# Four edits to the engines' order in the feed-forward part of a sandwich block: token split, second product's sum, third softmax group, rounding of the activations

## The chip, the cores and the metric

The program runs on 1 core of one Trainium2 chip. The metric is the device time of the whole program in microseconds (us), as a median of several executions. An execution that was profiled stands beside them, and every row of the trace comes from that one.

## What is computed

Two attention blocks on x of shape (2, 2048, 256), in float32, each with a residual and layer norms around it. The first is plain attention with 16 heads of 16. The second, in which the change lies, is a stack of two layers of this form (cut to what matters):

```python
def _layer(x, wqkv, qs, ksc, wo, lg, lb, w1, b1, w2, b2):
    h = shift_token(x)                       # half of the channels come from the token before
    q, k, v = split(h @ wqkv)                # 8 heads of 64
    q, k = rotary_xpos(l2norm(q) * qs, l2norm(k) * ksc)
    o = local_attention(q, k, v)             # windows of 128, each also sees the window before
    x = x + o @ wo
    h = shift_token(x)
    h = layer_norm(h) * lg + lb
    a, g = split(h @ w1 + b1)                # 682 wide each
    x = x + (a * gelu(g)) @ w2 + b2
    return x

for l in range(2): x = _layer(x, ...)
x = x + _layernorm(...)
```

## The kernel before

The program has a projection phase, the first attention (in which the scores, exponentials and maxima of 32 heads run for most of the first half of the time) and `feed_forward_phase`, which the change edits. It is written engine by engine: each engine has a list of its own, in program order, and semaphores between them. Nothing reorders them: an instruction that waits holds everything behind it on its engine.

The feed-forward phase works on 64 tiles of 128 tokens (32 in each of two layers, the two batches taking turns), as a software pipeline. In step t the engines work on several tiles at once: scores, softmax and attention of tile t+1, projection and rotary embedding of tile t+2, transposed tokens of tile t+3, the layer norm in the middle of tile t, and the hidden products of a pair of tiles. The steps alternate:

- In an **even step** (t even) TensorE makes the hidden layer of a pair, `hidden` (L1307), in two parts; ScalarE takes the gelu of it in six chunks (`gelu`, L1504 and L1506); VectorE multiplies each by the other half (`gated`, L1726); ScalarE rounds the product in two halves (`round_hidden`, L1515), and GpSimd makes the remainders (`split_hidden`, L1102).
- In an **odd step** TensorE makes the second product, `hidden_out` (L1379, L1380, L1386), for both tiles of the pair, and VectorE adds it to x (`add_hidden`, L1665), once early in the step and once at its end.

TensorE's list in a step is: `scores` (L1240), `hidden` chunks 0 to 2 or `hidden_out`, `project` (L1209), `transposed_probs` (L1279, four groups j = 0 to 3 of two heads each), `transposed_hidden_in` (L1255), `hidden` chunks 3 to 5 or `hidden_out`, `outputs_of_heads` (L1321), `transposed_q_k` (L1344), `attended` (L1360), `transposed_x` (L1193). Some of its waits matter here. `transposed_probs` waits for a group to be normalised, and before group 2 for both cosine products of the tile t+2 (`cos_done`, VectorE L1691), since the two share PSUM banks. `hidden_out` of the odd step's second half waits for VectorE's copy of the transposed group 1 (`copy_PT`, L1705). `attended` waits for ScalarE's `copy_oT` (L1520).

The softmax of a tile runs in four groups of 128x512: VectorE adds the mask and takes the maximum (`mask_and_maximum`, L1634), ScalarE the exponential with its sum (L1463), VectorE the reciprocal (`invert_sums`, L1642), and GpSimd (groups 0 and 1, L1054) or VectorE (groups 2 and 3, L1648) multiplies by it. `normalise_mid` (L1684) is the layer norm's scaling on VectorE, from SBUF to SBUF; `mean_and_variance` (L1672 to L1677) before it waits for a DMA that SyncE issues from the finished `x_mid` (L1732), which shifts the tokens by one. `split_xT` (L1653 and L1658) makes the remainder of the transposed tokens from ScalarE's rounded ones (`round_xT`, L1532 and L1534). `sines` (L1075), `inverse_norms` (L1083, L1085), `add_b2` (L1064), `inverse_deviation` (L1059) and `split_y` (L1093, L1095) are on GpSimd. ScalarE's `copy_projected` (L1474, L1475, L1477) gives the projected queries and keys to `sines` and their squares to VectorE.

Of the kernel before, what the change touches and what calls it, by code (L numbers as in the profile page):

```python
# [774 lines left out]
TILES = LAYERS * NT  # L775
# [85 lines left out]
def feed_forward_phase(nc, ins, weights, stacks, division, x_sb, outputs, spare, wo1_loaded, x1_dram, mask_sb, ident, out):  # L861

    with ExitStack() as ctx:
# [93 lines left out]
        exists = lambda v: 0 <= v < TILES  # L957
# [9 lines left out]
        def finished_pair(t):  # L967

            v = t - 5
            return v // 2 if v % 2 == 0 and NT * (LAYERS - 1) <= v < TILES else None  # L970
# [58 lines left out]
        def _(pool):  # L1029
# [31 lines left out]
            def add_b2(v):  # L1061

                pool.wait_ge(x_mid_made, v + 1)
                nc.gpsimd.tensor_tensor(out=x_sb[:, place(v)], in0=x_mid[:, v % 4, 0:2].rearrange("p a c -> p (a c)"), in1=b2_sb[:, layer(v)], op=ALU.add).then_inc(x_b2_made, 1)  # L1064
# [84 lines left out]
            for t in steps:  # L1149
                p = finished_pair(t - 1)  # L1150
                if p is not None:
                    add_x1(p - NT // 2)
                if exists(t + 1):
                    normalise(t + 1, 0)
                    normalise(t + 1, 1)
                if t == -1:
                    outputs_step(PAIRS1 + 1)
                if exists(t):
                    inverse_deviation(t)
                    add_b2(t)  # L1160
                if exists(t + 2):
                    sines(t + 2)
                if t == -1:
                    outputs_step(PAIRS1 + 2)
                if exists(t + 2):
                    inverse_norms(t + 2)
                if exists(t):
                    split_y(t)
                if t % 2 == 0 and exists(t - 2):
                    split_hidden((t - 2) // 2)  # L1170
                if exists(t + 3) and (t + 3) % 2 == 0:
                    rotary_tables((t + 3) // 2)
                p = finished_pair(t)
                if p is not None:
                    last_deviation(p - NT // 2)
# [3 lines left out]
        def _(pe):  # L1179
# [78 lines left out]
            def transposed_probs(v):  # L1258

                hidden_before = v % 2 == 0 and v >= 4  # L1260
                for j in range(4):
                    pe.wait_ge(normed_pool if j < 2 else normed_dve, 2 * v + j % 2 + 1)
                    if j == 0:
                        pe.wait_ge(max_made, 4 * v + 4)
                    if j == 1:
                        if hidden_before:
                            pe.wait_ge(act_made, HC * ((v - 4) // 2) + 5)
                        elif v >= 5:
                            pe.wait_ge(x_new, v - 3)
                        elif v:  # L1270
                            pe.wait_ge(PT_by_dve, 2 * (v - 1) + 1)
                        else:
                            pe.wait_ge(o_normed, 2 * (PAIRS1 - 2))
                    if j >= 2 and exists(v + 1):
                        pe.wait_ge(squares_made, 2 * (v + 1) + 4 - j)
                        pe.wait_ge(cos_done, 2 * (v + 1) + 4 - j)
                    for u in range(2):
                        for kb in key_blocks(v):
                            last = nc.tensor.transpose(bank[PT_BANK[j]][:, (2 * u + kb) * P:(2 * u + kb + 1) * P], probs[j][:, u, kb * P:(kb + 1) * P], ident[:])  # L1279
                    last.then_inc(PT_done, 1)  # L1280
# [172 lines left out]
        def _(act):  # L1453
# [119 lines left out]
            for t in steps:  # L1573
                if exists(t + 1):
                    exponentials(t + 1)
                if t == NT - 1:
                    act.wait_ge(Y_done, NT)
                    weights.load_wo(act, ins, 1)
                if t == NT + 1:
                    weights.load_w1(act, 1)  # L1580
                if t == NT + 2:
                    act.wait_ge(F_done, NT)
                    weights.load_w2(act, 1)
                if t == -1:
                    outputs_step(PAIRS1 + 1)
                if exists(t + 2):
                    copy_projected(t + 2)
                    if t == -1:
                        for k in range(PAIRS1 + 2, PAIRS1 + 5):
                            outputs_step(k)  # L1590
                    if t + 2 == NT - 1:
                        weights.load_second_wqkv(act)
                if exists(t + 1):
                    copy_PT(t + 1)
                if exists(t):
                    affine(t)
                if t % 2 == 0 and exists(t - 2):
                    gelu((t - 2) // 2)
                if exists(t + 1):
                    copy_oT(t + 1)  # L1600
                if exists(t + 2):
                    copy_qT_kT(t + 2)
                if t % 2 == 0 and exists(t - 2):
                    round_hidden((t - 2) // 2, 0)
                if t >= 0 and exists(t + 3):
                    round_xT(t + 3)
                if t % 2 == 0 and exists(t - 2):
                    round_hidden((t - 2) // 2, 1)
                p = finished_pair(t)
                if p is not None:  # L1610
                    normalise_last(p - NT // 2)

        @block.vector
        def _(dve):
# [189 lines left out]
                    scale_keys(0)  # L1804
            for t in steps:
                even, finished = t % 2 == 0, finished_pair(t)
                if exists(t + 1):
                    mask_and_maximum(t + 1, 0)
                    mask_and_maximum(t + 1, 1)
                if t >= 0 and exists(t + 2):  # L1810
                    split_xT(t + 2)
                if exists(t + 1):
                    mask_and_maximum(t + 1, 2)
                    invert_sums(t + 1, 0)
                    mask_and_maximum(t + 1, 3)
                    invert_sums(t + 1, 1)
                if t == -1:
                    outputs_step(PAIRS1 + 1)
                if not even and exists(t - 3):
                    add_hidden(t - 3)  # L1820
                if t == TILES - 1:
                    add_hidden(t - 2)
                if exists(t):
                    mean_and_variance(t)
                if exists(t + 1):
                    for j in (2, 3):
                        invert_sums(t + 1, j)
                        normalise(t + 1, j)
                if t == -1:
                    outputs_step(PAIRS1 + 2)  # L1830
                if exists(t + 2):
                    cosines(t + 2, 1)
                    square_norms(t + 2, 1)
                    cosines(t + 2, 0)
                if t == -1:
                    outputs_step(PAIRS1 + 3)
                    outputs_step(PAIRS1 + 4)
# [118 lines left out]
```

## Time and profile before

| what | value |
|---|---|
| time, median of 3 executions | 2870.36 us (2862.08 to 2893.25) |
| the profiled execution | 2864.45 us, its span 2862.7 us |
| busy TensorE | 2753.9 us, 96% |
| busy VectorE | 2324.5 us, 81% |
| busy ScalarE | 2151.1 us, 75% |
| busy GpSimd | 1133.5 us, 40% |

The feed-forward phase in its steady state begins at about 1640 us from the span's start and ends at about 2820 us. A row of the timeline gives an instruction's start and length; in square brackets stands how long its engine was idle before it, and what ended that. Rows of PEld are TensorE's weight loads, which overlap its matmuls. Line numbers are those of the kernel before.

### The profile page before, as it was taken

The page shows a single profiled execution, that of the slowest core. Times are in us where ns is not written, and L with a number is a line of the kernel's source. Part 1 is how long each engine was busy: PE and PEld are TensorE (multiplying, and loading weights), DVE is VectorE, ACT ScalarE, POOL GpSimd, SP SyncE. Part 2 cuts the span into 40 slices and gives each one's busy share as a digit, 9 for nine tenths or more (in the row PEclk, how much of TensorE's full clock was granted, in tenths as well). Part 3 has the DMA queues.
Part 4 walks back from the last instruction along what each step waited for, and adds up shares of the span by engine and source line. Part 5 has one row for each costly group of instructions (what it writes and reads, how often), then busy time and mean ns, then how long its engine had stood idle before and what let it go on. Part 6 is the DMA issues. An engine that isn't in the chain of part 4 may idle for free. (4 is left out here: it accounts for less than half of the span.)

```text
span 2862.7 us, 60523 instructions
## 1 busy us (share of the span) xinstructions
PE 2753.9 (96%) x22992; PEld 1747.6 (61%) x22992; DVE 2324.5 (81%) x4351; ACT 2151.1 (75%) x4620; POOL 1133.5 (40%) x1307
## 2 busy tenths in 40 slices
PE   7999999999999999999997899999999999999997
PEld 7733333333333333333346788888888888888886
DVE  6779999999999999999917677777777777777774
ACT  5568888888888888888875666677667777777774
POOL 7600000010001000010007666676667767777774
PEclk9979999999999999999999899999999999999999
DMA  5613333434442443344312100000001100000000
GB/s 167 192 18 53 48 51 56 68 60 68 63 75 55 68 63 66 58 74 64 69 32 82 64 5 7 7 6 7 5 7 58 68 14 20 21 21 13 21 19 25
DMA packets 92640, 138.76 MB, mean 48 GB/s; under 512 B 38529, under 2 KB 63041, under 8 KB 84929
## 3 DMA queue, kind: packets, MB, share of 16 engines
q1 hardware_dynamic: 86416, 125.40, 22.1%
q10 hardware_dynamic: 5936, 9.50, 1.0%
q8 instruction: 184, 3.01, 0.5%
q14 instruction: 104, 0.84, 0.1%
HBM read 88.17 MB, written 37.75 MB: 44 GB/s over the span
## 5 line engine op out<-in xcount | busy, mean ns | idle before, releaser
L684 ACT ACTIVATE probs<-scores 128x512 f32<-128x512 f32 x2048 | 1114.3, 597 | 204.0 <-PE scores L610 81.4
L717 DVE TENSOR_REDUCE mx<-aux 128x1 f32<-128x1024 f32 x982 | 1200.8, 1223 | 66.1 <-PE aux L578 58.8
L578 PE MATMUL aux<-k_stack,q_stack 48*128 48x512 f32 x2006 | 751.1, 450 | 14.1 <-DVE mx L725 7.7
L610 PE MATMUL scores<-q_stack,k_stack 50*128 50x512 f32 x2048 | 764.0, 451 | 0.0
L623 PE MATMUL pv<-probs,v_ones 128*32 128x256 f32 x8192 | 659.9, 394 | 0.1
L610 PEld LDWEIGHTS scores<-q_stack,k_stack 50*128 50x128 f32 x2048 | 311.0, 186 | 429.9 <-ACT probs L684 412.4
L623 PEld LDWEIGHTS pv<-probs,v_ones 128*32 128x32 f32 x8192 | 161.9, 108 | 362.0 <-ACT probs L684 288.3
L531 POOL CAST m_parts<-head_max 128x16 fp32r<-128x16 f32 x32 | 6.3, 196 | 877.3 <-DVE head_max L710 877.3
L578 PEld LDWEIGHTS aux<-k_stack,q_stack 48*128 48x128 f32 x2006 | 303.0, 187 | 43.4 <-DVE mx L717 21.3
L1463 ACT ACTIVATE VO<-VO,tables_small 128x256 f32<-128x256 f32 (+1 forms) x512 | 250.5, 491 | 41.4 <-DVE tables_small L1634 41.1
L1307 PE MATMUL bank<-q_minus_first,q_stack 128*128 128x256 f32 x2112 | 271.4, 287 | 2.2 <-POOL q_minus_first L1095 2.2
L1307 PEld LDWEIGHTS bank<-q_minus_first,q_stack 128*128 128x128 f32 x2112 | 259.3, 193 | 12.5 <-issue 9.9
L1209 PE MATMUL bank<-wqkv_hi,k_stack 128*128 128x512 f32 x768 | 253.3, 397 | 7.9 <-DVE tables_small L1634 5.3
L1634 DVE CUSTOM_DVE_ANT_0 VO<-bank,mask_sb,tables_small 128x256 f32<-128x256 f32 (+1 forms) x512 | 216.1, 469 | 52.0 <-PE bank L1240 52.0
L1085 POOL TENSOR_TENSOR tables_small<-tables_small 128x8 f32<-128x8 f32 x128 | 220.8, 1725 | 10.7
L1075 POOL TENSOR_TENSOR VO<-VO,tables_small 128x512 f32<-128x512 f32 x128 | 162.8, 1294 | 91.0 <-issue 90.9
L1054 POOL TENSOR_TENSOR VO<-VO,tables_small 128x512 f32<-128x512 f32 (+1 forms) x128 | 127.2, 1014 | 153.9 <-DVE tables_small L1642 153.9
L1209 PEld LDWEIGHTS bank<-wqkv_hi,k_stack 128*128 128x128 f32 x768 | 145.4, 189 | 40.3 <-issue 5.5
L1732 DVE TENSOR_TENSOR x_mid<-bank,x_sb 128x256 f32<-128x256 f32 x64 | 27.2, 424 | 160.1 <-PE bank L1360 160.1
L1279 PE MATMUL bank<-ident,VO 128*128 128x128 f32 x992 | 126.1, 274 | 29.0 <-DVE VO L1691 28.6
L1209 PE MATMUL bank<-wqkv_lo,k_stack 128*128 128x512 f32 x384 | 152.0, 396 | 0.0
L1102 POOL TENSOR_TENSOR k_stack<-gate,k_stack 128x768 fp32r<-128x768 f32 x64 | 116.8, 1846 | 87.8 <-ACT k_stack L1515 87.8
(178 smaller groups left out, 4559.2 us busy)
## 6 DMA issues: line engine op xcount, KB each, us to landing
q_stack<-qk_dram SPq DMA_DIRECT2D x192, 128.0 KB, 4.9
k_stack<-qk_dram SPq DMA_DIRECT2D x192, 128.0 KB, 6.9
qk_dram<-qkT_hi SPq DMA_DIRECT2D x32, 256.0 KB, 3.6
qk_dram<-qkT_lo SPq DMA_DIRECT2D x32, 256.0 KB, 3.9
w_parts<-weight_pieces SPq DMA_DIRECT2D x28, 256.0 KB, 2.4
VO<-o_stage SPq DMA_DIRECT2D x128, 32.0 KB, 6.9
q_minus_first<-sums_dram SPq DMA_DIRECT2D x32, 128.0 KB, 2.9
x_dram<-x_sb SPq DMA_DIRECT2D x16, 256.0 KB, 2.0
```

The lines of the kernel that those rows point to most:

```text
L578: return nc.tensor.matmul(out, q_stack[max_rows, n % BODY, tile * P:(tile + 1) * P], k_stack[max_rows, n % BODY, keys * 512:(keys + 1) * 512],
L610: last = nc.tensor.matmul(out, k_stack[0:SCORE_ROWS, n % BODY, s * P:(s + 1) * P], q_stack[0:SCORE_ROWS, n % BODY, j * 512:(j + 1) * 512], ...
L623: last = nc.tensor.matmul(pv[VW * j:VW * (j + 1), columns], v_ones[:, n % BODY, s, :], probs[:, (BLOCKS * step + j) % PROBS, columns], sta ...
L684: nc.scalar.activation(probs[:, e % PROBS], scores[:, item_of_exp(e) % BANKS1], ACT.Exp, scale=float(D1) ** -0.5).then_inc(act_emptied, 1)
L717: nc.vector.tensor_reduce(mx[:, n % BODY, tile, half:half + 1], aux[:, unit % 2].rearrange("p a k -> p (a k)"), AX.X, ALU.max).then_inc(dv ...
L1054: nc.gpsimd.tensor_tensor(out=p4, in0=p4, in1=rsums[:, j].unsqueeze(2).to_broadcast([P, 2, P * len(key_blocks(v))]), op=ALU.mult).then_inc ...
L1075: last = nc.gpsimd.tensor_tensor(out=o4[:, :, :, lo:lo + D2 // 2], in0=q4[:, :, :, hi:hi + D2 // 2], in1=sin_table[:, v // 2 % 2, :, lo:lo ...
L1085: nc.gpsimd.tensor_tensor(out=rnorm[:, v % 2, heads], in0=norm2_min[:, heads], in1=minus_half[:, heads], op=ALU.pow).then_inc(rnorm_made, 1)
L1209: last = nc.tensor.matmul(bank[QKV_BANK[a]][:], x_part[:, v % 4, k, tokens], w_part[:, k, columns], start=(k == 0 and n == 0), stop=(k == ...
L1307: last = nc.tensor.matmul(out_half, w_part[:, k, chunk * P:(chunk + 1) * P], h_part[:, p % 2, k], start=(k == 0 and n == 0), stop=(k == NC ...
L1463: last = nc.scalar.activation(probs[j][:, u, keys], probs[j][:, u, keys], ACT.Exp, scale=-1.0, bias=negmax[:, j, u:u + 1], accum_out=sums[ ...
L1634: last = nc.vector.tensor_tensor_reduce(out=probs[j][:, u, at:at + n_keys], in0=src[:, 2 * u * P + at:2 * u * P + at + n_keys], in1=mask_s ...
```

## The change

Four edits of order, one of them with a change of engine:

- `split_xT` of tile t+2 goes in front of all of VectorE's masks and maxima; it stood behind the second of four.
- The first `add_hidden` of an odd step goes behind the two cosine products and the first sum of squares; it stood in front of `mean_and_variance`.
- Group 2 of the softmax is normalised by GpSimd, behind `inverse_deviation`; VectorE keeps group 3 alone. `add_b2` goes behind `sines`.
- Both halves of `round_hidden` go right behind `gelu`, in front of `copy_oT` and the copies of q and k; they stood behind those, the one in front of `round_xT`, the other behind it.

```diff
@@ GpSimd, step t
                 if exists(t):
                     inverse_deviation(t)
-                    add_b2(t)
+                if exists(t + 1):
+                    normalise(t + 1, 2)
                 if exists(t + 2):
                     sines(t + 2)
+                if exists(t):
+                    add_b2(t)
@@ TensorE, transposed_probs
-                    pe.wait_ge(normed_pool if j < 2 else normed_dve, 2 * v + j % 2 + 1)
+                    pe.wait_ge(normed_pool if j < 3 else normed_dve, 3 * v + j + 1 if j < 3 else v + 1)
@@ ScalarE, step t
                     gelu((t - 2) // 2)
+                if t % 2 == 0 and exists(t - 2):
+                    for i in range(2):
+                        round_hidden((t - 2) // 2, i)
                 if exists(t + 1):
                     copy_oT(t + 1)
                 if exists(t + 2):
                     copy_qT_kT(t + 2)
-                if t % 2 == 0 and exists(t - 2):
-                    round_hidden((t - 2) // 2, 0)
                 if t >= 0 and exists(t + 3):
                     round_xT(t + 3)
-                if t % 2 == 0 and exists(t - 2):
-                    round_hidden((t - 2) // 2, 1)
@@ VectorE, step t
+                if t >= 0 and exists(t + 2):
+                    split_xT(t + 2)
                 if exists(t + 1):
                     mask_and_maximum(t + 1, 0)
                     mask_and_maximum(t + 1, 1)
-                if t >= 0 and exists(t + 2):
-                    split_xT(t + 2)
-                if exists(t + 1):
                     mask_and_maximum(t + 1, 2)
                     invert_sums(t + 1, 0)
                     mask_and_maximum(t + 1, 3)
                     invert_sums(t + 1, 1)
-                if not even and exists(t - 3):
+                if t == TILES - 1:
                     add_hidden(t - 3)
-                if t == TILES - 1:
                     add_hidden(t - 2)
                 if exists(t):
                     mean_and_variance(t)
                 if exists(t + 1):
-                    for j in (2, 3):
-                        invert_sums(t + 1, j)
-                        normalise(t + 1, j)
+                    invert_sums(t + 1, 2)
+                    invert_sums(t + 1, 3)
+                    normalise(t + 1, 3)
                 if exists(t + 2):
                     cosines(t + 2, 1)
                     square_norms(t + 2, 1)
                     cosines(t + 2, 0)
+                if not even and t != TILES - 1 and exists(t - 3):
+                    add_hidden(t - 3)
```

The order of three engines at the places in question, with what each instruction waits for. First ScalarE in an even step before, from the last full gelu chunk to the load of the exponentials' table (`k_stack` is here the memory in which the rounded activations and the transposed tokens lie, `VO` holds the keys):

```order
L1504 ACTIVATE gate3<-bank3,b1_sb 128x256 [waits H_done]
L1506 ACTIVATE gate3<-bank4,b1_sb 64x256 [waits H_done]
L1520 COPY oT3<-bank5 128x512 [waits oT_done]
L1525 COPY qT3<-bank6 128x512 [waits qkT_done]
L1527 COPY VO<-bank0 128x512 [waits qkT_done]
L1515 CAST k_stack<-gate3 128x768 [waits F_done,act_made]
L1532 CAST k_stack<-bank2 128x2x128 [waits xT_done]
L1534 CAST k_stack<-bank2 128x1
L1515 CAST k_stack<-gate3 128x768 [waits act_made]
L1463 ACT_TABLE_LOAD
```

The same place of the changed kernel, whose line numbers are 3 higher here:

```order
L1507 ACTIVATE gate3<-bank3,b1_sb 128x256 [waits H_done]
L1509 ACTIVATE gate3<-bank4,b1_sb 64x256 [waits H_done]
L1518 CAST k_stack<-gate3 128x768 [waits F_done,act_made]
L1518 CAST k_stack<-gate3 128x768 [waits act_made]
L1523 COPY oT3<-bank5 128x512 [waits oT_done]
L1528 COPY qT3<-bank6 128x512 [waits qkT_done]
L1530 COPY VO<-bank0 128x512 [waits qkT_done]
L1535 CAST k_stack<-bank2 128x2x128 [waits xT_done]
L1537 CAST k_stack<-bank2 128x1
L1466 ACT_TABLE_LOAD
```

The copy of oT now stands behind two roundings, each of which waits for VectorE's products (`act_made`).

VectorE in an odd step before, from the first `add_hidden` to the copy of the transposed group 1:

```order
L1665 TENSOR_TENSOR x_sb<-bank0,x_sb 128x256 [waits x_b2_made,F_done]
L1672 BN_STATS tables_small3<-x_mid 128x6 [waits shifted1,x_mid_made]
L1672 BN_STATS tables_small3<-x_mid 128x6
L1675 BN_AGGR tables_small3<-tables_small3 128x2 [waits hstats_made]
L1677 TENSOR_SCALAR tables_small3<-tables_small3 128x1 [waits hmv_made]
...
L1648 TENSOR_TENSOR VO<-VO,tables_small3 128x512 [waits rsums3_made]
L1691 TENSOR_TENSOR VO<-bank5,tables_small3 128x512 [waits squares_made,rotary_tables_made]
L1699 TENSOR_REDUCE tables_small3<-VO 128x8 [waits norm2_floor_made,squares_made]
L1691 TENSOR_TENSOR VO<-bank4,tables_small3 128x512 [waits squares_made]
L1684 TENSOR_SCALAR wo1_bo1_sb<-x_mid,tables_small3 128x256 [waits hT_done,hrstd_made]
L1705 COPY PT3<-bank3 128x512 [waits PT_done]
```

And in the changed kernel, whose line numbers are 2 higher here:

```order
L1674 BN_STATS tables_small3<-x_mid 128x6 [waits shifted1,x_mid_made]
L1674 BN_STATS tables_small3<-x_mid 128x6
L1677 BN_AGGR tables_small3<-tables_small3 128x2 [waits hstats_made]
L1679 TENSOR_SCALAR tables_small3<-tables_small3 128x1 [waits hmv_made]
...
L1650 TENSOR_TENSOR VO<-VO,tables_small3 128x512 [waits rsums3_made]
L1693 TENSOR_TENSOR VO<-bank5,tables_small3 128x512 [waits squares_made,rotary_tables_made]
L1701 TENSOR_REDUCE tables_small3<-VO 128x8 [waits norm2_floor_made,squares_made]
L1693 TENSOR_TENSOR VO<-bank4,tables_small3 128x512 [waits squares_made]
L1667 TENSOR_TENSOR x_sb<-bank0,x_sb 128x256 [waits x_b2_made,F_done]
L1686 TENSOR_SCALAR wo1_bo1_sb<-x_mid,tables_small3 128x256 [waits hT_done,hrstd_made]
L1707 COPY PT3<-bank3 128x512 [waits PT_done]
```

The sum with the second product (L1665, now L1667) moved from the head of this stretch to a place between the cosines and the scaling of the layer norm.

GpSimd in an odd step before, from the softmax groups to the inverse norms:

```order
L1054 TENSOR_TENSOR VO<-VO,tables_small3 128x512 [waits rsums3_made] x2
L1059 TENSOR_TENSOR tables_small3<-tables_small3 128x1 [waits var3_made]
L1064 TENSOR_TENSOR x_sb<-x_mid,q_minus_first 128x256 [waits x_mid_made]
L1075 TENSOR_TENSOR VO<-VO,tables_small3 128x16x32 [waits rot3_made,qk3_copied,rotary_tables_made]
L1075 TENSOR_TENSOR VO<-VO,tables_small3 128x16x32
L1083 TENSOR_SCALAR tables_small3<-tables_small3 128x8 [waits norm2_made]
```

And in the changed kernel:

```order
L1054 TENSOR_TENSOR VO<-VO,tables_small3 128x512 [waits rsums3_made] x2
L1059 TENSOR_TENSOR tables_small3<-tables_small3 128x1 [waits var3_made]
L1054 TENSOR_TENSOR VO<-VO,tables_small3 128x512 [waits rsums3_made]
L1075 TENSOR_TENSOR VO<-VO,tables_small3 128x16x32 [waits rot3_made,qk3_copied,rotary_tables_made]
L1075 TENSOR_TENSOR VO<-VO,tables_small3 128x16x32
L1064 TENSOR_TENSOR x_sb<-x_mid,q_minus_first 128x256 [waits x_mid_made]
L1083 TENSOR_SCALAR tables_small3<-tables_small3 128x8 [waits norm2_made]
```

A third product of 128x512 stands ahead of the sines, and the sum with b2 behind them.

## Rows read from the trace of the kernel before

**Rows 1.** Windows view: PE, PEld, DVE, ACT, POOL busy us (instructions), PE clock, DMA share, GB/s.

```profile
1740.00:2000.00 260.00, 254.75 (x2006) 225.03 (x2006) 193.09 (x564) 184.07 (x460) 177.92 (x182) 1.00 0.02 6
```

**Rows 2.** Waits, 1750 to 2750 us: total, times, longest, in us.

```profile
PE bank L1279 <- DVE VO L1691: 17.8, 26, 1.0
...
PEld bank L1379 <- DVE PT L1705: 9.4, 24, 0.4
```

**Rows 3.** Timeline, TensorE, an even step: start, length in us.

```profile
2026.78 1.91 PE L1279 MATMUL bank<-ident,VO 128*128 128x128 f32 x16
...
2035.25 1.89 PE L1360 MATMUL bank<-wo_sb,oT 128*128 128x256 f32 x8
...
2037.29 2.00 PE L1240 MATMUL bank<-VO,qT 64*128 64x256 f32 x16
```

**Rows 4.** Timeline, ScalarE, the same even step and the next step's begin.

```profile
2025.59 0.59 ACT L1474 COPY VO<-bank 128x512 f32<-128x512 f32 x1 [0.30 <-PE bank L1209]
...
2033.02 0.47 ACT L1506 ACTIVATE gate<-bank,b_sb 64x256 f32<-64x256 f32 x1
2034.44 0.59 ACT L1520 COPY oT<-bank 128x512 f32<-128x512 f32 x1 [0.95 <-PE bank L1321]
...
2037.72 0.84 ACT L1515 CAST k_stack<-gate 128x768 fp32r<-128x768 f32 x1
2038.58 1.28 ACT L1463 ACT_TABLE_LOAD   x1
```

**Rows 5.** Timeline, VectorE, the same even step.

```profile
2027.31 0.43 DVE L1684 TENSOR_SCALAR wo_bo_sb<-x_mid,tables_small 128x256 f32<-128x256 f32 x1
...
2031.57 1.26 DVE L1726 SCALAR_TENSOR_TENSOR gate<-bank,b_dve,gate 128x256 f32<-128x256 f32 x3 [0.64 <-ACT gate L1504]
...
2033.36 1.25 DVE L1726 SCALAR_TENSOR_TENSOR gate<-bank,b_dve,gate 128x256 f32<-128x256 f32 x3
```

**Rows 6.** Timeline, TensorE, the odd step behind it.

```profile
2045.65 1.04 PE L1279 MATMUL bank<-ident,VO 128*128 128x128 f32 x8
2047.37 1.07 PE L1279 MATMUL bank<-ident,VO 128*128 128x128 f32 x8 [0.68 <-DVE VO L1691]
2048.27 0.38 PE L1255 MATMUL bank<-ident,wo_bo_sb 128*128 128x128 f32 x2
2048.80 0.39 PE L1379 MATMUL bank<-w_hi,k_stack 128*128 128x256 f32 x1
```

**Rows 7.** Timeline, VectorE, the same odd step.

```profile
2042.56 0.48 DVE L1672 BATCH_NORM_STATS2 tables_small<-x_mid 128x6 f32<-128x128 f32 x2
...
2044.39 1.04 DVE L1648 TENSOR_TENSOR VO<-VO,tables_small 128x512 f32<-128x512 f32 x1
...
2046.54 0.68 DVE L1691 TENSOR_TENSOR VO<-bank,tables_small 128x512 f32<-128x512 f32 x1
2047.14 1.00 DVE L1684 TENSOR_SCALAR wo_bo_sb<-x_mid,tables_small 128x256 f32<-128x256 f32 x1
2048.07 0.68 DVE L1705 COPY PT<-bank 128x512 f32<-128x512 f32 x1
```

**Rows 8.** Timeline, VectorE around the shifting DMA: even step, then odd.

```profile
2016.15 0.42 DVE L1732 TENSOR_TENSOR x_mid<-bank,x_sb 128x256 f32<-128x256 f32 x1 [3.68 <-PE bank L1360]
...
2021.53 0.49 DVE L1672 BATCH_NORM_STATS2 tables_small<-x_mid 128x6 f32<-128x128 f32 x2 [0.25 <-DMA x_mid<-x_mid]
...
2037.18 0.42 DVE L1732 TENSOR_TENSOR x_mid<-bank,x_sb 128x256 f32<-128x256 f32 x1 [2.58 <-PE bank L1360]
```

**Rows 9.** Timeline, GpSimd, the same odd step.

```profile
2041.53 2.04 POOL L1054 TENSOR_TENSOR VO<-VO,tables_small 128x512 f32<-128x512 f32 x2 [0.87 <-DVE tables_small L1642]
...
2044.06 0.82 POOL L1064 TENSOR_TENSOR x_sb<-x_mid,q_minus_first 128x256 f32<-128x256 f32 x1
2045.49 2.50 POOL L1075 TENSOR_TENSOR VO<-VO,tables_small 128x512 f32<-128x512 f32 x2 [0.61 <-issue]
```

**Rows 10.** Timeline, ScalarE, the same odd step.

```profile
2044.79 0.57 ACT L1474 COPY VO<-bank 128x512 f32<-128x512 f32 x1
```

## The prediction, made before the changed kernel ran

> **What bounds the kernel now.** I first read the table of busy time by stretch: in a steady stretch of 260 us TensorE is busy for 254.75, at the full granted clock of 2.4 GHz, and VectorE, the next, for 193.09 [rows 1]. So TensorE's list is the time of this phase, and an edit counts only by what it adds to or takes from TensorE's own waits. The table of waits shows how little there is to take: 17.8 us in 26 places behind VectorE's second cosine product, and 9.4 in 24 places (weight loads) behind VectorE's copy of the transposed group [rows 2]. I then read the timeline of one pair of steps, engine by engine. The pattern repeats through both layers, so two steps carry the whole sum.
>
> In the even step TensorE has no wait: its 16 transposes of the probabilities run through in one piece [rows 3]. In the odd step it stops twice. The last eight of these transposes begin 1.72 us behind the first eight (2045.65 to 2047.37), where half of the even step's uninterrupted piece of 1.91 is about 0.87 with the overlap taken off, which leaves 0.85 of waiting; then the second product begins at 2048.80, 0.53 behind the layer norm's transposes, of which some 0.15 is work, so 0.38 is waiting [rows 3, 6]. Together 1.23 us in each pair is the most that the edits can win, over 31 pairs 38 us.
>
> **Rounding ahead of oT's copy: a new wait in the even step.** The second rounding waits for all six products of `gated`. VectorE ends them at 2033.36 + 1.25 = 2034.61 [rows 5], and what sets that is gelu, which the change leaves where it is. ScalarE ends gelu at 2033.49 [rows 4]. So its new list reads: first rounding 2033.5 to 2034.33 (0.84 each) [rows 4], idle until 2034.65, second rounding to 2035.48, copy of oT (0.59) from about 2035.4 or 2035.5 to 2036.0 or 2036.1. Before, this copy began at 2034.44 and ended at 2035.03 [rows 4], and TensorE began `attended` at 2035.25 straight behind its transposes [rows 3]: 0.22 of slack. With a tenth of a us from ScalarE's end to TensorE's start, `attended` begins at 2036.1 to 2036.2: a loss of 0.82 to 0.95, I take 0.9. Nothing catches it: queued behind `attended` on TensorE are the transposed tokens and the next tile's scores (2037.29) [rows 3], and on VectorE x_mid, the shifting DMA behind it on SyncE's queue and the next masks; all move by as much. The copies of q and k move too, but scores have over a us of their own in hand. The next step's hidden_out gets its rounded input earlier, for which it hardly waits now.
>
> What this edit gives back: the second rounding (0.84) no longer stands between the transposed tokens and the table load of 1.28 [rows 4], so in the odd step, counted from its scores, the exponentials can begin up to 0.5 us earlier and the copy of the queries after them. But that copy can't come earlier than TensorE's projection. In the even step, where it does wait for it, it begins 1.19 ahead of the first transposes (2025.59 against 2026.78) [rows 3, 4]; in the odd step it begins 0.86 ahead (2044.79 against 2045.65) [rows 6, 10]. It can win 0.33 and no more.
>
> **Third group on GpSimd, and the first `add_hidden` behind the cosines.** VectorE loses a product of 128x512 ahead of its cosines (0.68 for one of that size, or 1.04) [rows 7] and the sum, whose like of 128x256 takes 0.42 [rows 8]. With that the second cosine product in the odd step ends about 0.8 to 0.9 us earlier from the scores: it is then bound by ScalarE's squares. This is enough for the first of the two waits, all 0.85 of it. The group itself isn't late: GpSimd's products take 1.02 each [rows 9], the third is done some 0.8 us behind the end of `inverse_deviation`, well over a us ahead of its transposes.
>
> The second wait grows instead. What it waits for is VectorE's chain `normalise_mid`, copy of group 1. `normalise_mid` takes 0.43 in the even step and 1.00 in the odd [rows 5, 7], and in the odd one ends at 2048.14, 0.15 behind GpSimd's sines (2045.49 + 2.50 = 2047.99) [rows 9]. I read this as follows: it can't run beside the second of the two sine instructions and ends when that is over. The sines start 0.13 behind the queries' copy (2044.79 + 0.57 = 2045.36), so by the 0.33 above they move by 0.3 and no more, and `normalise_mid` with them: `add_hidden` now stands directly in front of it and keeps it from slipping in before the second sine instruction begins. Counted from the scores at 2037.29: the queries' copy begins at 7.50 - 0.33 = 7.17 and takes 0.57, their squares as long again, to 8.3; the second cosine product (0.68) ends at 9.0, `add_hidden` at 9.35, when `normalise_mid` could start; the second sine instruction begins at 8.20 - 0.33 + 1.25 = 9.12. So it ends at about 10.5 against 10.85 now, the copy of group 1 as much earlier, and the second product starts 0.35 earlier, not 1.23. If the third product on GpSimd pushes the sines by 0.1, it is 0.25. I take 0.3.
>
> The Trainium skill, in "SBUF — State Buffer", section "Who interferes with whom", says that VectorE in a mode with two ports, or with two SBUF inputs, and GpSimd share a port pair, that whoever starts first has it for the whole instruction, and that the other blocks. The 1.00 and the 1.04 rows agree with it. Taken strictly it would let VectorE's group 3 hold off GpSimd's group 2 by 0.3, with the sines then 0.2 later than I have them; the boundary between the two sine instructions would fall on the very moment at which `normalise_mid` is ready. That is the second rival below, whose price is worked out there from rows.
>
> **`split_xT` in front.** Its cover is VectorE's idle time ahead of the masks; ScalarE's rounding is done early enough. The 0.40 that the masks gain comes to nothing, since `mean_and_variance` waits for the shifting DMA. In the even step it begins 2021.53 - 2016.57 = 4.96 us behind x_mid's end, and waits for it; in the odd step 2042.56 - 2037.60 = 4.96 as well [rows 7, 8]: the DMA is already the last there. So neither this nor `add_hidden`'s removal moves the mean; I cost it at nothing, and if the cover were gone it would cost the 0.40 in one step. `add_b2` (0.82) [rows 9] now stands ahead of the inverse norms, which end about half a us later from the scores; the scaling of the keys on VectorE needs the first of them and is busy until then. In the last layer the final deviation is as much later, and with it x_mid of an odd step, but the even step that follows has no wait on TensorE to lengthen.
>
> **The sum.** A pair: + 0.9 - 0.3 = + 0.6 us. 31 pairs: + 18.6. The first steps, which have no hidden products, wait longer for the cosines and should win 1 or 2 us in all. That makes + 17 us. On the profiled execution's 2864.45 that is 2881.5; the median of the three runs stands 5.9 above that execution, which gives 2887. I name 2884, between them. By the bound of 1%, about what a measurement of this kernel can tell from no change (28.7 us), this is no change, on the slow side.
>
> **The rivals.** (a) *Nothing is won in the odd step.* If VectorE's last product is held by GpSimd's third, as its 1.04 row beside GpSimd's sum with b2 shows it can be [rows 7, 9], the cosines end where they did; or `normalise_mid` waits for sines that come 0.3 later. It decides against me if GpSimd's third product starts before VectorE's. For it: they are within 0.4 us of each other. Against: in the row before, VectorE's started first and kept its length. Then the loss stands alone: 31 x 0.82 to 0.95 = + 25 to + 29, 2890 to 2899. (b) *`normalise_mid` slips in between the sine instructions*, as it does in the even step with 0.43. It misses by 0.2 us by my sum. Then the second wait falls to 0.1 or so, 1.1 is won, and a pair gains 0.2: 31 x 0.2 = - 6, with the first steps - 8, 2856 to 2863. (c) *ScalarE's order costs nothing*, because VectorE's products end sooner than now and oT's copy stays in its slack. Against: gelu sets them. Then the odd step's 0.3 to 1.23 in each pair is all gain: 2826 to 2855. (d) *The new orders stall elsewhere*, in the last layer above all, where GpSimd has most to do: + 30 to + 45, 2894 to 2915.
>
> **Chances.** Forecast (+ 8 to + 24) 0.50, (a) 0.22, (b) 0.17, (c) 0.05, (d) 0.06. The range takes the forecast, (a) and (b): 2856 to 2902; the forecast's own is 2872 to 2894. Over 1% faster is only the far half of (c): 0.03. Over 1% slower is (d) and the upper end of (a) with a median that lies high: 0.15. Within 1%: 0.82.
>
> **What the profile after would show.** Right: in even steps a wait of TensorE in front of `attended` for the copy of oT, some 0.9 us, 31 times; in odd steps no wait for the cosines, and one of 0.7 to 0.9 in front of the layer norm's transposes and the second product; `normalise_mid` at 1 us or more in odd steps; an idle time of 0.6 ahead of the mean, ended by the DMA; a pair of steps at 40.3 us where it is 39.7. Wrong: no such wait in front of `attended`, which would mean that the products end sooner; `normalise_mid` at 0.43 in odd steps, which is (b); or a second cosine product that ends no earlier from the scores than 9.9 us, which is (a).

## The result and the profile after

| | kernel before | changed kernel |
|---|---|---|
| median | 2867.75 us (20 runs) | 2888.09 us (20 runs) |
| ratio | 1 | 1.0071, 95% interval 1.0056 to 1.0085 |
| the profiled execution's span | 2862.7 us | 2884.1 us |

The change makes the kernel slower by 0.7%: some 20 us, 21.4 between the two spans. A ratio is always one of executions in the chip's faster state, which leaves out one of the ten of e3 below (2896.79 us). First the page of the changed kernel, its busy times:

```profile
PE 2767.0 (96%) x22992; PEld 1751.0 (61%) x22992; DVE 2276.4 (79%) x4287; ACT 2155.9 (75%) x4620; POOL 1205.7 (42%) x1371
```

VectorE has 48 us less to do and GpSimd 72 more, with the same instructions on TensorE. None of that says where the time went. The table of waits does (1750 to 2750 us: total, times, longest, in us), against [rows 2]:

```profile
PEld bank L1363 <- ACT oT L1523: 24.8, 25, 1.8
PE bank L1363 <- ACT oT L1523: 18.8, 25, 1.6
...
PEld bank L1258 <- DVE wo_bo_sb L1686: 15.2, 25, 0.9
...
PE bank L1258 <- DVE wo_bo_sb L1686: 9.2, 25, 0.7
PEld bank L1382 <- DVE PT L1707: 9.6, 24, 0.4
```

A wait of TensorE can stand there twice, once for its matmuls (PE) and once for the weight loads ahead of them (PEld); the two are not to be added. The 17.8 us that TensorE waited for the second cosine product are gone but for 0.8. In their place stand two other waits: for oT's copy, once in each even step (25 in this stretch), and for the layer norm's scaling, once in each odd step. The wait for the copy of the transposed group is as it was. The timeline of one even step and the odd step behind it shows them in place, TensorE first, against [rows 3, 6]:

```profile
2039.96 1.09 PE L1347 MATMUL bank<-ident,VO 128*128 128x128 f32 x8
2041.77 1.99 PE L1363 MATMUL bank<-wo_sb,oT 128*128 128x256 f32 x8 [0.72 <-ACT oT L1523]
...
2043.91 2.00 PE L1243 MATMUL bank<-VO,qT 64*128 64x256 f32 x16
...
2052.25 1.97 PE L1282 MATMUL bank<-ident,VO 128*128 128x128 f32 x16
2054.58 0.44 PE L1258 MATMUL bank<-ident,wo_bo_sb 128*128 128x128 f32 x2 [0.35 <-DVE wo_bo_sb L1686]
...
2062.36 2.00 PE L1243 MATMUL bank<-VO,qT 64*128 64x256 f32 x16
```

`attended` (L1363) begins 1.81 us behind the transposes of q and k, where it was 0.92 (2034.33 to 2035.25). The odd step's 16 transposes now run in one piece, but the layer norm's begin 2.33 behind them, where the even step needs 1.75. ScalarE in the same even step, against [rows 4]:

```profile
2038.65 0.47 ACT L1509 ACTIVATE gate<-bank,b_sb 64x256 f32<-64x256 f32 x1
2039.15 0.83 ACT L1518 CAST k_stack<-gate 128x768 fp32r<-128x768 f32 x1
2040.27 0.83 ACT L1518 CAST k_stack<-gate 128x768 fp32r<-128x768 f32 x1 [0.30 <-DVE gate L1728]
2041.13 0.58 ACT L1523 COPY oT<-bank 128x512 f32<-128x512 f32 x1
```

The first rounding follows gelu almost at once, the second waits 0.30 us for VectorE's last products, and oT's copy, whose input was there at 2039.96 or so, starts at 2041.13. Then the odd step, VectorE and GpSimd, against [rows 5, 7, 9]:

```profile
2049.16 0.49 DVE L1674 BATCH_NORM_STATS2 tables_small<-x_mid 128x6 f32<-128x128 f32 x2 [0.61 <-DMA x_mid<-x_mid]
...
2050.29 0.69 DVE L1650 TENSOR_TENSOR VO<-VO,tables_small 128x512 f32<-128x512 f32 x1
...
2052.33 0.68 DVE L1693 TENSOR_TENSOR VO<-bank,tables_small 128x512 f32<-128x512 f32 x1
2052.93 0.41 DVE L1667 TENSOR_TENSOR x_sb<-bank,x_sb 128x256 f32<-128x256 f32 x1
2053.26 1.26 DVE L1686 TENSOR_SCALAR wo_bo_sb<-x_mid,tables_small 128x256 f32<-128x256 f32 x1
2054.44 0.68 DVE L1707 COPY PT<-bank 128x512 f32<-128x512 f32 x1
```

```profile
2050.67 1.21 POOL L1054 TENSOR_TENSOR VO<-VO,tables_small 128x512 f32<-128x512 f32 x1
2051.85 2.53 POOL L1075 TENSOR_TENSOR VO<-VO,tables_small 128x512 f32<-128x512 f32 x2
2054.32 0.78 POOL L1064 TENSOR_TENSOR x_sb<-x_mid,q_minus_first 128x256 f32<-128x256 f32 x1
```

The cosines end 9.1 us behind the scores (2053.01 - 2043.91) where they ended 9.9 behind. The sum takes its 0.41, and the scaling (L1686) starts at 2053.26, when the second sine instruction has just begun (2051.85 + 1.26 = 2053.11, half of the row). It lasts 1.26 us and ends 0.14 behind the sines.

I took the start of every tile's scores from the two timelines. From the first step with hidden products on, 28 of the 30 even steps are 0.98 us longer than before, and 28 of the 30 odd ones shorter by 0.22 to 0.30: 22.02 for 21.04 and 18.45 for 18.70. All 30 even steps together are longer by 29.9, the 30 odd ones shorter by 7.4, and the first three steps shorter by 1.4. That makes 21.1 us between the first scores and the last.

The two odd ones out among the even steps: at the border of the two layers one loses 1.96 instead of 0.98. Its tile is the first of a batch and sees one block of keys only, and the wait for oT's copy is the longest there (1.6 on TensorE); that oT is ready earlier against gelu in such a tile is my reading. And one step loses only 0.44, since the kernel before lost 0.54 in it (21.58 for 21.04). There the layer norm's scaling began 0.03 us before the end of the first sine instruction and waited out the second, for 1.41 us instead of the even step's 0.43.

### The profile page after: what moved, and what is told of

Its sections match the earlier page's. It is cut to its first block and busy times, and to the rows that moved or that the text cites. A ratio compares the mean times of both kernels' runs of the same rounds, so it can differ in the third digit from the quotient of the medians.

```text
span 2884.1 us, 60523 instructions
## 1 busy us (share of the span) xinstructions
PE 2767.0 (96%) x22992; PEld 1751.0 (61%) x22992; DVE 2276.4 (79%) x4287; ACT 2155.9 (75%) x4620; POOL 1205.7 (42%) x1371
## 5 line engine op out<-in xcount | busy, mean ns | idle before, releaser
L1054 POOL TENSOR_TENSOR VO<-VO,tables_small 128x512 f32<-128x512 f32 (+1 forms) x192 | 201.2, 1061 | 191.9 <-DVE tables_small L1644 191.7
L1085 POOL TENSOR_TENSOR tables_small<-tables_small 128x8 f32<-128x8 f32 x128 | 241.9, 1890 | 10.7
L1363 PE MATMUL bank<-wo_sb,oT 128*128 128x256 f32 x512 | 125.5, 388 | 23.8 <-ACT oT L1523 23.8
L1693 DVE TENSOR_TENSOR VO<-bank,tables_small 128x512 f32<-128x512 f32 x128 | 88.0, 688 | 62.8 <-ACT VO L1478 57.6
```

What stands on the lines that cost most here:

```text
L1054: nc.gpsimd.tensor_tensor(out=p4, in0=p4, in1=rsums[:, j].unsqueeze(2).to_broadcast([P, 2, P * len(key_blocks(v))]), op=ALU.mult).then_inc ...
L1085: nc.gpsimd.tensor_tensor(out=rnorm[:, v % 2, heads], in0=norm2_min[:, heads], in1=minus_half[:, heads], op=ALU.pow).then_inc(rnorm_made, 1)
L1363: last = nc.tensor.matmul(bank[Y_BANK][:, 0:C], oT[:, c], wo_sb[:, c], start=(c == 0), stop=(c == 3))
```

## The experiments

Each variant was timed against the kernel before on the same chip: e1 to e4 on one, where that took 2868.06 us, e5 to e8 on another, where it took 2865.70. So compare ratios, not times. e2, e4, e7 and e8 have 4 executions, the others 10. "Steps" are the distances between the scores of successive tiles in the profiled execution, even and odd.

A ratio of so few executions is blunt beside an edit worth a few us, for much of the spread arises ahead of the changed phase: the first scores begin between 1550.9 us (e8) and 1565.7 (e2), and the mean granted clock in the first 1550 us is 0.99 in the one and 0.97 in the other. From 1600 to 2750 us it is 1.00 in every profile. So the time from the first scores to the last, read in each profile, shows the edits more sharply:

| kernel | first scores to last, us | against before |
|---|---|---|
| before | 1252.4 | |
| changed | 1273.5 | + 21.1 |
| e1 | 1251.5 | - 0.9 |
| e2 | 1275.2 | + 22.8 |
| e3 | 1243.4 | - 8.9 |
| e4 | 1217.6 | - 34.8 |
| e5 | 1249.4 | - 3.0 |
| e6 | 1244.7 | - 7.7 |
| e7 | 1217.4 | - 35.0 |
| e8 | 1231.5 | - 20.9 |

**e1: roundings back.** All of the change but ScalarE's part:

```diff
-                if t % 2 == 0 and exists(t - 2):
-                    for i in range(2):
-                        round_hidden((t - 2) // 2, i)
                 if exists(t + 1):
                     copy_oT(t + 1)
                 if exists(t + 2):
                     copy_qT_kT(t + 2)
+                if t % 2 == 0 and exists(t - 2):
+                    round_hidden((t - 2) // 2, 0)
                 if t >= 0 and exists(t + 3):
                     round_xT(t + 3)
+                if t % 2 == 0 and exists(t - 2):
+                    round_hidden((t - 2) // 2, 1)
```

> The changed kernel with ScalarE's list as before (both roundings behind the copies again); the other three edits stay. Theory (the wait for oT's copy is the whole loss, and the 0.24 us won in odd steps came from ScalarE's side): no wait in front of the attended product, an even step of 21.03 us, and an odd step of 18.69, because the queries' copy and with it the sines come where they came before; only the first steps win. So 0.999 of the kernel before, 0.992 of the changed one. Rival (GpSimd's third product and the blocked scaling make the loss): 1.005 or more of the kernel before. Second rival (the two VectorE edits win the odd step by themselves): odd steps of 18.4, 0.996.

Measured: 0.9994 (0.9971 to 1.0016), steps 21.04 and 18.71. Both rivals fall: without ScalarE's edit nothing is lost, and VectorE's and GpSimd's edits win nothing by themselves. The odd step's wait is in front of the transposes again, for the second cosine product, as in the kernel before (waits of this kernel, 1750 to 2750 us):

```profile
PE bank L1282 <- DVE VO L1694: 22.2, 26, 0.9
```

The lighter list of VectorE did not bring the cosines forward here, and VectorE's and GpSimd's timelines of an odd step show why:

```profile
2044.62 1.47 DVE L1651 TENSOR_TENSOR VO<-VO,tables_small 128x512 f32<-128x512 f32 x1
```

```profile
2044.51 1.04 POOL L1054 TENSOR_TENSOR VO<-VO,tables_small 128x512 f32<-128x512 f32 x1
```

ScalarE's exponentials come later than in the changed kernel, and VectorE waits 0.44 us for the sums of the last group. GpSimd's third product then starts first, by 0.11 us, and VectorE's takes 1.47 us instead of 0.69. This is the mechanism of the forecast's rival (a), and it comes in every odd step of this kernel in which a tile sees two blocks (1.45 to 1.49 us). The second cosine product ends 10.1 us behind the scores, where it ended 9.9 behind. The sines start 8.20 behind the scores, as before, so the scaling ends where it did.

**e2: roundings alone.** The kernel before with only ScalarE's edit (the diff above, read backwards).

> The kernel before with the roundings in front of oT's copy as the only edit. Theory: even steps of 22.02 us (+ 0.99), and odd steps won 0.25 to 0.35 by the earlier sines although VectorE's list is as before, since the scaling of the layer norm ends with the sines either way: 1.007 to 1.008 of the kernel before, the same as the changed kernel. Rival (the odd step is won by VectorE's shorter list): odd steps stay at 18.69, 1.011.

Measured: 1.0091 (1.0061 to 1.0120), steps 22.02 and 18.50. The loss of the even step is whole with this edit alone, and 0.20 of the odd step's gain comes with it, although VectorE's list is that of before. The ratio lies a little above my 1.008, within its interval. The odd step of this kernel on VectorE and on GpSimd:

```profile
2065.34 0.81 DVE L1683 TENSOR_SCALAR wo_bo_sb<-x_mid,tables_small 128x256 f32<-128x256 f32 x1
2066.07 0.68 DVE L1704 COPY PT<-bank 128x512 f32<-128x512 f32 x1
```

```profile
2063.28 2.71 POOL L1075 TENSOR_TENSOR VO<-VO,tables_small 128x512 f32<-128x512 f32 x2 [0.22 <-issue]
```

The scaling ends at 2066.15, again 0.16 behind the sines (2065.99).

**e3: one rounding ahead.** The changed kernel, but only the first rounding stands ahead of oT's copy; the second stands behind the copies of q and k:

```diff
                 if t % 2 == 0 and exists(t - 2):
-                    for i in range(2):
-                        round_hidden((t - 2) // 2, i)
+                    round_hidden((t - 2) // 2, 0)
                 if exists(t + 1):
                     copy_oT(t + 1)
                 if exists(t + 2):
                     copy_qT_kT(t + 2)
+                if t % 2 == 0 and exists(t - 2):
+                    round_hidden((t - 2) // 2, 1)
                 if t >= 0 and exists(t + 3):
                     round_xT(t + 3)
```

> The changed kernel with only the first rounding in front of oT's copy; the second goes behind the copies of q and k and in front of the tokens' rounding. Theory: the first rounding ends before oT is there, so the wait goes (even step 21.03), while the exponentials' table load still comes early and the odd step keeps its 0.24 (18.45): 31 x 0.24 and the first steps, 0.996 to 0.997 of the kernel before. Rival (oT's copy is late by the first rounding too, or the tokens' rounding is now late): even steps of 21.3 or more, 1.000 or above.

Measured: 0.9968 (0.9949 to 0.9986), steps 21.04 and 18.44. As the theory had it. From 1750 to 2750 us TensorE waits for oT once, for 0.3 us, at the border of the layers. There the first rounding alone is in the way of oT's copy too, and the step takes 19.54 us instead of 18.84.

**e4: one rounding ahead, late sum.** As e3, with the first `add_hidden` of an odd step moved once more (VectorE's list, cut to what matters):

```diff
                     cosines(t + 2, 0)
-                if not even and t != TILES - 1 and exists(t - 3):
-                    add_hidden(t - 3)
                 if exists(t):
                     normalise_mid(t)
                 if exists(t + 1):
                     copy_PT(t + 1, 1)
                 if exists(t + 2):
                     square_norms(t + 2, 0)
                 if exists(t + 1):
                     copy_PT(t + 1, 3)
+                if not even and t != TILES - 1 and exists(t - 3):
+                    add_hidden(t - 3)
```

> As the one before, and the first add_hidden of an odd step stands behind the copy of the transposed group 3, no longer between the cosines and the layer norm's scaling. Theory (the scaling is stuck behind the second sine instruction because it comes 0.15 us too late): it now starts before that instruction, takes 0.3 to 0.45 us, and the second wait of the odd step goes as well: odd steps of 17.5 to 17.8 us, 0.984 to 0.988 of the kernel before. Rival (the scaling takes 1.0 to 1.26 in odd steps whenever the sines run, wherever it starts): odd steps of 18.4, as the one before.

Measured: 0.9888 (0.9853 to 0.9923), median 2839.72 us, steps 21.03 and 17.6 in the first layer, 17.5 in the second. The steps are those of the theory. The ratio lies just above the 0.984 to 0.988 that I expected, with most of that range inside its interval, and the 34.8 us between the scores are 1.2%. The scaling now starts before the first of the two sine instructions is over, on VectorE and GpSimd (an odd step, whose scores began at 2021.74):

```profile
2030.16 0.68 DVE L1694 TENSOR_TENSOR VO<-bank,tables_small 128x512 f32<-128x512 f32 x1
2030.75 0.40 DVE L1687 TENSOR_SCALAR wo_bo_sb<-x_mid,tables_small 128x256 f32<-128x256 f32 x1
2031.17 0.69 DVE L1708 COPY PT<-bank 128x512 f32<-128x512 f32 x1
```

```profile
2029.67 2.62 POOL L1075 TENSOR_TENSOR VO<-VO,tables_small 128x512 f32<-128x512 f32 x2
```

It takes 0.40 us where it took 1.26, and TensorE runs from its transposes into the second product without a wait:

```profile
2030.10 1.95 PE L1282 MATMUL bank<-ident,VO 128*128 128x128 f32 x16
2031.89 0.38 PE L1258 MATMUL bank<-ident,wo_bo_sb 128*128 128x128 f32 x2
2032.02 0.37 PE L1382 MATMUL bank<-w_hi,k_stack 128*128 128x256 f32 x1
```

**e5: late sum, both roundings ahead.** The changed kernel with the sum moved as in e4.

> The changed kernel with both roundings in front of oT's copy, and the first add_hidden of an odd step behind the copy of the transposed group 3. Theory (the two waits are independent): even steps of 22.02 us as in the changed kernel, odd steps of 17.5 to 17.6: a pair is 0.1 us shorter than before, 0.995 to 0.997 of the kernel before. Rival (the early input of the second product, or something else that the roundings' place brings, is needed for the short odd step, or the late one spoils it): odd steps of 18 or more, 1.001 or above.

Measured: 1.0006 (0.9983 to 1.0029), steps 22.02 and 17.5 to 17.6. The steps are those of the theory; the two waits are independent, and each edit adds its own. The wait for oT in the even step costs here nearly all that the late sum wins in the odd one. My ratio of 0.995 to 0.997 did not follow from my own steps: 0.1 us in 31 pairs and the first steps are some 4 us, 0.998 to 0.999. Between the first scores and the last 3.0 us are won, 0.999, because the border of the layers loses 3.6 us (22.40 for 18.84). In that step the eight matmuls of `attended` take 3.40 us behind their wait, for a cause that I did not look for.

**e6: third group back on VectorE**, on top of e4 (cut; TensorE's waits for the groups go back with it):

```diff
# GpSimd
-                if exists(t + 1):
-                    normalise(t + 1, 2)
# VectorE
-                    invert_sums(t + 1, 2)
-                    invert_sums(t + 1, 3)
-                    normalise(t + 1, 3)
+                    for j in (2, 3):
+                        invert_sums(t + 1, j)
+                        normalise(t + 1, j)
```

> The fast variant (one rounding ahead, late sum) with group 2 normalised by VectorE again. Theory: VectorE's 0.62 us more ahead of the cosines bring the layer norm's scaling to 9.6 us behind the scores, past the begin of the second sine instruction at 9.1, so it is stuck to 10.4 again: odd steps of 18.3 to 18.45, 0.997 of the kernel before. Rival (the third group on GpSimd does nothing, the late sum is all): odd steps of 17.6, 0.989.

Measured: 0.9988 (0.9966 to 1.0010), steps 21.04 and 18.36 in the first layer, 18.5 in the second; the 7.7 us won between the scores are the 0.997 expected. So the third group on GpSimd is worth about 0.8 to 1.0 us in an odd step on top of e4: without it the scaling comes too late again. VectorE's scaling and GpSimd's sines in an odd step of this kernel are

```profile
2008.77 1.02 DVE L1685 TENSOR_SCALAR wo_bo_sb<-x_mid,tables_small 128x256 f32<-128x256 f32 x1
```

```profile
2007.13 2.52 POOL L1075 TENSOR_TENSOR VO<-VO,tables_small 128x512 f32<-128x512 f32 x2 [1.04 <-issue]
```

The second sine instruction began at about 2008.39, and the scaling came 0.38 us later and paid 0.6 us. In one odd step, which took 18.66 us instead of 18.36, it came 0.06 us behind that boundary and took 1.34 us.

**e7: `split_xT` back**, on top of e4, behind the second of the four masks.

> The fast variant with split_xT behind the second of the four masks again. Theory (the shifting DMA ends the wait for the mean, so the 0.40 us fall into it): no change against the fast variant, steps of 21.03 and 17.5 to 17.6, 0.989 of the kernel before; VectorE's idle time in front of the mean falls from 0.61 to about 0.2. Rival (the early remainders or maxima are used): odd steps of 17.9 to 18.0, 0.993.

Measured: 0.9886 (0.9861 to 0.9911), steps 21.03 and 17.5 to 17.6: no difference to e4 (35.0 us won between the scores, 34.8 in e4). VectorE's wait for the DMA ahead of the mean falls from the 0.61 of the changed kernel to

```profile
2049.27 0.49 DVE L1675 BATCH_NORM_STATS2 tables_small<-x_mid 128x6 f32<-128x128 f32 x2 [0.23 <-DMA x_mid<-x_mid]
```

**e8: `add_b2` back in front of the sines**, on top of e4:

```diff
-                if exists(t + 2):
-                    sines(t + 2)
                 if exists(t):
                     add_b2(t)
+                if exists(t + 2):
+                    sines(t + 2)
```

> The fast variant with add_b2 in front of the sines again, so that the sines start 0.75 to 0.8 us later. Theory (the scaling can't run beside a sine instruction and ends some 0.15 us behind the one it meets): it now meets the first of the two, which ends 9.9 us behind the scores, and takes about 1.0 us; the second product starts 0.35 to 0.4 later: odd steps of 17.9 to 18.0, 0.993 of the kernel before. Rival (its long time in the odd step has another cause, such as its own input or the DMA): it takes 0.4 as in the fast variant, odd steps of 17.5 to 17.6.

Measured: 0.9923 (0.9892 to 0.9953), steps 21.04 and 17.9 in the first layer, 18.06 in the second. The scaling and the sines:

```profile
2034.54 1.06 DVE L1687 TENSOR_SCALAR wo_bo_sb<-x_mid,tables_small 128x256 f32<-128x256 f32 x1
```

```profile
2034.15 2.58 POOL L1075 TENSOR_TENSOR VO<-VO,tables_small 128x512 f32<-128x512 f32 x2
```

The first sine instruction ends at about 2035.44, the scaling at 2035.60. With VectorE's list unchanged from e4, only the time at which GpSimd starts its sines moved, and the same VectorE instruction went from 0.40 to 1.06 us.

## Why the prediction was right

The forecast was + 17 us, 2884; measured were 2888 and a ratio of 1.0071, + 20 us. By its own steps:

- **The new wait for oT's copy: right, a little small.** I had `attended` late by 0.9 us (0.82 to 0.95). It is late by 0.89, and the step is longer by 0.98: behind the wait the eight matmuls of `attended` take 1.99 us instead of 1.89. Before, their first weight load began 0.11 us ahead of the first matmul, under the transposes; now both begin at 2041.77. The forecast left out that tenth, 3 us in all. e2 shows the wait by this edit alone, e3 that it goes in the steady steps when only the second rounding goes back. What set it was read rightly: the second rounding waits for the last products, which gelu sets.
- **The odd step wins 0.3, not 1.23: right.** It won 0.25. The first wait went, as forecast, and came back in front of the layer norm's transposes. The scaling was forecast to be ready 0.2 us too late and missed by 0.15. So the second product begins 2.93 us behind the step's first transposes, where it was 3.15 and where e4 needs 1.92 without a wait: of the 1.23 us some 1.0 is left. The sines moved by 0.26 and not 0.3, since GpSimd's third product took 1.21 and not 1.02.
- **What GpSimd's third product costs.** I named 0.1 us as its possible push of the sines; it is 0.08. VectorE's product of group 3 (2050.29, 0.69) started first and kept its length, and GpSimd's, which began 0.38 later, was longer by 0.19. The Trainium skill ("SBUF — State Buffer", "Who interferes with whom") says that the one which starts first has the shared pair and the other blocks; this trace agrees in who pays, and by 0.19 of the 0.31 us in which the two overlapped. In e1 the order is the other way round, and so is who pays: VectorE's product is longer by 0.78 of an overlap of 0.93.
- **`split_xT` in front at nothing: right**, by e7. VectorE's wait for the DMA took the 0.40 (0.61 against 0.23).
- **The first steps: 1.4 us, where I had 1 or 2.** The border of the layers, with another 1 us of loss, was not foreseen.
- **The rivals.** (a) did not come, as VectorE's product started first; but e1 shows that this hangs on ScalarE's edit, without which GpSimd's starts first and the cosines gain nothing. The forecast had named GpSimd's earlier start as the danger, but not that ScalarE's roundings decide which of the two starts first. (b), the scaling slipping in between the sine instructions, did not come in the changed kernel but is real: e4 puts it there by moving one sum and the second rounding, and wins 1.1% against the kernel before; e3 to e4, the sum alone, is 0.9 us in each odd step. (c) is refuted by e2. Of (d) nothing was seen.

That the odd step's win comes from ScalarE's edit, by way of the sines, and not from VectorE's lighter list, was in the forecast's working but not drawn out as a claim. e1 and e2 show it: VectorE's and GpSimd's edits without ScalarE's leave the odd step at 18.71; ScalarE's without them make it 18.50. The prediction came out right by its mechanism; that its total is short by 3 to 4 us comes from a loss and a gain that were each off by less than 0.1 us a pair, to the same side, and from the border.

So three of the four edits are sound or harmless once ScalarE's exponentials come early, and the change loses by one of its two roundings and by the place of one sum. With both put right (e4) the same change is a gain of 1.1%, and nearly all that I had counted of TensorE's waits in the steady pair is gone: 1.1 to 1.2 us of the 1.23.

## What to carry to other kernels

When the bounding engine waits twice in a row, removing the first wait is worth little until the chain behind the second has moved too: find what ends that one (here the sines on GpSimd, through the scaling on VectorE) before an edit is priced. In a list that nothing reorders, an instruction that waits for another engine must not be put ahead of a copy that the bounding engine needs, however much earlier its own result would be welcome; splitting the moved work, so that only the half whose input is there goes ahead, kept the gain without the loss. And VectorE instructions that can't run beside GpSimd's are priced by where they fall: 0.15 us late cost 0.9. That makes an edit's worth hang on the others: the third group on GpSimd won nothing in e1, where it started 0.11 us ahead of VectorE's product, and 0.8 to 1.0 us an odd step in e4.

## What the runs showed of the hardware

The scaling, an instruction from SBUF to SBUF of 128x256 with two scalar columns, shows the time of the GpSimd instruction that it meets. In the ten profiles, 64 scalings each, it took 0.40 us in the three cases in which GpSimd had nothing under way. Where it began 0.26 us or more before the end of the GpSimd instruction under way, it ended 0.14 to 0.16 us behind that, 531 times of 531: 0.43 in even steps, and in odd ones 0.81 (e2), 1.00 [rows 7], 1.02 (e6), 1.06 (e8) and 1.26 (the changed kernel). Where it began less than 0.14 us before that end it missed the gap and waited out the next sine instruction in ten cases of twelve, for 1.41 to 1.51 us. The length in a profile's row is then waiting for the most part, and no view counts it as idle.

Two products of 128x512 with both inputs in SBUF, one on VectorE and one on GpSimd, lengthen the one that starts later by most of the overlap: GpSimd's by 0.19 of 0.31 us (the changed kernel), VectorE's by 0.78 of 0.93 (e1). VectorE's 1.04 beside GpSimd's sum with b2 is the same in small: 0.34 more than the 0.70 of the product before it, of an overlap of 0.49 [rows 7, 9].

`attended`, begun behind a wait, costs about 0.1 us beyond the wait itself (1.99 against 1.89 us for eight matmuls of 128x256), 25 times in 25 in the stretch read.
